# A two-layer network on one core: in each slot of the first layer, 16-block inverses go through DRAM, and decay products take two heads at once

## The reference, cut to what matters

```python
def step(S, inp):
    q_t, k_t, v_t, a_t, b_t = inp
    kS = jnp.einsum('bhd,bhdv->bhv', k_t, S)
    kkS = jnp.einsum('bhd,bhv->bhdv', k_t, kS)
    S = a_t[..., None, None] * (S - b_t[..., None, None] * kkS) + jnp.einsum('bhd,bhv->bhdv', k_t, v_t)
    o_t = jnp.einsum('bhdv,bhd->bhv', S, q_t)
    return (S, o_t)
```

## Time and profile before

| What | Value |
| --- | --- |
| Median of 3 runs | 1298.65 us |
| Lowest and highest run | 1297.44 and 1306.99 us |
| Profiled execution, span from first to last instruction | 1268.3 us |
| Profiled execution, own time outside the span | not given apart from the runs |
| Median less span | 30.35 us |

### The profile page before, as it was taken

The page is one execution under the profiler, slowest core; times in us unless marked ns, Lnnn a source line. Parts: engine busy times, 40 slices in busy tenths (PEclk is TensorE's granted clock), DMA queues, the critical chain, the costliest instruction groups (busy, mean ns, idle before and its releaser), DMA issues.

```text
span 1268.3 us, 36893 instructions
## 1 busy us (share of the span) xinstructions
PE 1107.3 (87%) x14528; PEld 793.9 (63%) x14528; DVE 906.1 (71%) x1818; ACT 797.2 (63%) x1467; POOL 595.0 (47%) x1213
## 2 busy tenths in 40 slices
PE   5768899999999999999989989986878877998991
PEld 1113576676677677677677677775545444798990
DVE  4865789998899999899977877884457566251232
ACT  3756888888998898897876766753334333332330
POOL 2434467667567667667655755654010005004404
PEclk9878999999999999999999999997699888998996
DMA  7012222222222212222223222412001104398982
GB/s 248 1 43 69 54 72 54 55 68 60 52 66 54 58 48 77 53 56 71 54 48 90 54 63 63 71 33 31 8 14 22 30 7 140 113 301 272 337 291 54
DMA packets 131662, 106.33 MB, mean 84 GB/s; under 512 B 60113, under 2 KB 119377, under 8 KB 131233
## 3 DMA queue, kind: packets, MB, share of 16 engines
q1 hardware_dynamic: 129440, 99.76, 27.9%
q0 software_dynamic: 2048, 4.20, 1.0%
HBM read 84.06 MB, written 15.73 MB: 79 GB/s over the span
## 4 chain that ended last, share of the span: by engine, by line
PE 51%; DVE 22%; issue 11%; POOL 6%; ACT 5%; DMA 2%; SPq 2%; DVEq 0%; POOLq 0%; ACTq 0%
PE bank L1052 6%; PE pair L732 5%; DVE vc L1499 4%; PE bank L1006 3%; PE bank L1059 3%; DVE AM L1569 3%; PE pair L696 3%; DVE kc L1499 3%; PE bank L834 2%; PE bank L784 2%; POOL xs L2007 2%; PE bank L879 2%; PE pair L850 2%; PE bank L773 2%; PE bank L826 2%
## 5 line engine op out<-in xcount | busy, mean ns | idle before, releaser
L1953 POOL TENSOR_TENSOR SU<-SU 128x14 f32<-128x14 f32 (+6 forms) x448 | 161.5, 360 | 34.9
L1957 POOL TENSOR_TENSOR SU<-SU 128x14 f32<-128x14 f32 (+6 forms) x448 | 147.5, 329 | 35.1
L1499 DVE SCALAR_TENSOR_TENSOR vc<-vy,conv,vc 128x512 f32<-128x512 f32 x192 | 152.2, 793 | 13.9 <-ACT vc L1194 13.5
L1499 DVE SCALAR_TENSOR_TENSOR kc<-ky,conv,kc 128x512 f32<-128x512 f32 x162 | 126.9, 808 | 10.7 <-ACT kc L1168 9.8
L2033 POOL TENSOR_TENSOR RR<-RR,nh 128x8 f32<-128x8 f32 x32 | 65.2, 2036 | 138.6 <-DVE RR L1641 138.5
L1839 DVE TENSOR_TENSOR vy<-bank,vc 128x512 f32<-128x512 f32 x46 | 31.8, 692 | 98.7 <-PE bank L1052 97.5
L732 PE MATMUL pair<-SM,KQ 64*128 64x128 f32 (+1 forms) x512 | 74.8, 369 | 18.1 <-DVE AM L1569 14.1
L1929 POOL TENSOR_TENSOR st<-st,nh 128x4 f32<-128x4 f32 x16 | 19.0, 1186 | 120.0 <-DVE st L1475 111.2
L696 PE MATMUL pair<-xnT,WQ 128*128 128x512 f32 x128 | 74.3, 663 | 0.2 <-DVE SM L1518 0.2
L664 PE MATMUL pair<-xnT,WQ 128*128 128x512 f32 x128 | 72.7, 653 | 1.5 <-ACT xnT L1156 0.8
L1802 DVE TENSOR_REDUCE SM<-pair 128x4 f32<-128x1024 f32 x32 | 39.1, 1222 | 41.5 <-PE pair L964 40.5
(11 more groups left out here) (315 smaller groups left out, 3190.6 us busy)
## 6 DMA issues: line engine op xcount, KB each, us to landing
AM<-in_wex_dram SPq DMA_DIRECT2D x32, 768.0 KB, 5.5
SM<-dscr SPq DMA_DIRECT2D x58, 256.0 KB, 3.7
V<-in_wex_dram SPq DMA_DIRECT2D x14, 768.0 KB, 5.0
et<-dscr SPq DMA_DIRECT2D x38, 256.0 KB, 3.7
SM<-fscr SPq DMA_DIRECT2D x64, 128.0 KB, 3.0
scratch<-AM SPq DMA_DIRECT2D x128, 48.0 KB, 1.8
SU<-scratch SPq DMA_DIRECT2D x256, 15.5 KB
xs<-idle SPq DMA_DIRECT2D x2, 1472.0 KB, 9.2
```

The costliest lines, as they stand in the source:

```text
L1499: e.scalar_tensor_tensor(c, y[:, :, k:k + 256], conv[:, ct, k:k + 1], c, ALU.mult, ALU.add).then_inc(s_c, 1)
L1953: e.tensor_tensor(tmp[:, 0:k, 0:15 - k], sub[:, 0:k, k:k + 1].to_broadcast([128, k, 15 - k]), sub[:, k:k + 1, k + 1:16].to_broadcast([128, ...
L1957: e.tensor_tensor(sub[:, 0:k, k + 1:16], sub[:, 0:k, k + 1:16], tmp[:, 0:k, 0:15 - k], ALU.subtract).then_inc(s_su, 1)
```

## The change

Four edits to the first layer's slot:

1. **Turning by DMA.** `inv_turn` and `inv_y0` go. SyncE gets `turned(n)`: it waits for the end of `substitute(n)` (and for the Y0 transfers of the unit before), writes SU's blocks to a new DRAM tensor `yscr` with 4 transfers, waits until they have landed, and reads them back into Y0 with 8 transfers, two for each group of 32 partitions. The reads fill only the diagonal 16-blocks of Y0, so the rest must be zero: a memset of Y0's second half is added to `substitute` ahead of step k = 7. It waits for `inv_w0` of the unit before. `turned(n - 1)` stands between `exponents(n + 1)` and `blocks(n)`. `inv_x0` waits for the 8 reads, and moves down behind the first tap of `vconv(2g + 1)`.
2. **Decay products of both heads at once.** The PSUM banks are renumbered so that banks 1 and 3 are the halves of one PSUM tensor, and `am` becomes three instructions of 128 x 1024 elements instead of six of 128 x 512. All waits on its semaphore are renumbered.
3. **The doubled copy on ScalarE.** `inv_w0` becomes two scaled copies of 128 x 256 elements on ScalarE, placed after `u2`. `inv_p1` becomes a multiplication of half as many elements by a number per partition. Masks shrink, and signs are moved so that `inv_s0` adds.
4. **GpSimd's order.** `scaled(g + 1)` always stands inside `substitute(g)`, ahead of k = 11, and so does a norm's power, where there is one, ahead of k = 9.

The small rest: one input fewer, two setup semaphores merged, two more memsets before the loop, and waits of the second layer's first units named anew for the renumbered banks.

```diff
-        bank = [D2[i // 2][:, 512 * (i % 2):512 * (i % 2) + 512] for i in range(4)]
+        bank = [D2[i % 2][:, 512 * (i // 2):512 * (i // 2) + 512] for i in range(4)]
...
-        NSU = 29
+        NSU = 30
...
             def blocks(n, new):
 
-                e.wait_ge(s_am, 6 * n + 6)
+                e.wait_ge(s_am, 3 * n + 3)
...
                 if n:
-                    e.wait_ge(s_i0, 3 * n - 2)
+                    e.wait_ge(l_y0, 128 * n)
...
+            def turned(n):
+
+                e.wait_ge(s_su, NSU * n + NSU)
+                if n:
+                    e.wait_ge(l_y0, 128 * n)
+                for a in range(4):
+                    e.dma_start(yscr[a], sub[32 * a:32 * a + 16, :, :]).then_inc(l_yw, 16)
+                e.wait_ge(l_yw, 64 * n + 64)
+                for a in range(4):
+                    for h in range(2):
+                        e.dma_start(Y0[32 * a + 16 * h:32 * a + 16 * h + 16, :, 16 * h:16 * h + 16],
+                                    yscr[a, 8 * h:8 * h + 8].rearrange("j r t -> r j t")).then_inc(l_y0, 16)
...
                 if n + 1 < NN: exponents(n + 1)
+                if n: turned(n - 1)
                 blocks(n, new and n + 1 < NN)
...
+            turned(NN - 1)
             for t in range(NTICK):
...
+            def inv_w0(n):
+                e.wait_ge(s_iy, 2 * n + 1)
+                if n:
+                    e.wait_ge(s_yfd, n)
+                e.activation(YP[:, :, 0:32], Y0[:, :, :], ACT.Copy, scale=minus_even32)
+                e.activation(YP[:, :, 32:64], Y0[:, :, :], ACT.Copy, scale=minus_odd32).then_inc(s_w0, 1)
...
-            def am(n, i):
-                part, hh = i // 2, i % 2
+            def am(n, part):
...
             def inv_x0(n):
-                e.wait_ge(s_i0, 3 * n + 2)
+                e.wait_ge(l_y0, 128 * n + 128)
                 e.transpose(X0[:, :, :], Y0[:, :, :]).then_inc(s_ix, 1)
...
             def inv_p1(n):
                 e.wait_ge(s_ia, 2 * n + 2)
-                e.tensor_tensor(PP[:, :, :], wide(bank[4]), lmask[:, :].unsqueeze(1).to_broadcast([128, NJ, 64]), ALU.mult).then_inc(s_ip, 1)
+                e.tensor_scalar(PP[:, :, 0:32], wide(bank[4])[:, :, 0:32], odd32, None, ALU.mult).then_inc(s_ip, 1)
...
                 for k in range(14, 0, -1):
-                    if late and k == 11:
+                    if k == 11 and n + 1 < NN:
                         scaled(n + 1)
+                    if k == 9 and key is not None:
+                        norm(key)
+                    if k == 7:
+                        if n:
+                            e.wait_ge(s_w0, n)
+                        c += 1
+                        e.memset(Y0[:, :, 16:32], 0.0).then_inc(s_su, 1)
```

More of the change, by code:

```diff
@@ L82, in program @@
         PP0 = sb("PP0", [128, NJ, 32])
-        bmask = sb("bmask", [128, 97])
-        mask16, mask32, odd16 = bmask[:, 0:32], bmask[:, 32:96], bmask[:, 96:97]
+        bmask = sb("bmask", [128, 5])
+        odd16, even16, odd32, minus_even32, minus_odd32 = (bmask[:, k:k + 1] for k in range(5))
         idle = sb("idle", [128, 512], BF16)
@@ L731, in gram @@
                             moved = KQ[hp:hp + 64, m, b, 1, s0:256] if k else KT2[hp:hp + 64, n % 2, b, s0:256]
-                            ins = e.matmul(bank[(3, 1)[hh]][:, part], KQ[hp:hp + 64, m, b, 0, s0:s0 + 128], moved, start=True, stop=True)
+                            ins = e.matmul(bank[2 * hh + 1][:, part], KQ[hp:hp + 64, m, b, 0, s0:s0 + 128], moved, start=True, stop=True)
                 ins.then_inc(s_gk, 1)
@@ L1437, in _ @@
                 if has_j: u2(j)
+                if has_i: inv_w0(i)
                 more(s, 7)
@@ L1896, in _ @@
                 if has_g: vconv(2 * g + 1, 0)
+                if has_i: inv_x0(i)
                 if has_e: lengths1(s // NG)
@@ L1905, in _ @@
                 if has_g: vconv(2 * g + 1, 2)
-                if has_i: inv_w0(i)
                 if has_i: inv_x1(i)
@@ L1938, in _, with substitute @@
             e.memset(PP0[:, :, :], 0.0).then_inc(s_zero, 1)
-            e.wait_ge(s_zero, 4)
-            def substitute(n, late):
+            e.memset(PP[:, :, :], 0.0).then_inc(s_zero, 1)
+            e.memset(Y0[:, :, :], 0.0).then_inc(s_zero, 1)
+            e.wait_ge(s_zero, 6)
+            def substitute(n, key):
                 c = NSU * n
@@ L2033, in _ @@
                     e.tensor_tensor(RR[:, 1, :, :], RR[:, 0, :, :], nh[:, :].rearrange("p (t h) -> p t h", t=4), ALU.pow).then_inc(s_r2, 1)
-                late = (g + 1) % NG == 0 and g + 1 < NN
-                if g + 1 < NN and not late: scaled(g + 1)
                 if s == 34:
@@ L2054, in _ @@
                     ins.then_inc(s_one, 1)
-                if gap(s + 1, "norm") is not None:
-                    norm(gap(s + 1, "norm"))
-                if g < NN: substitute(g, late)
+                if g < NN: substitute(g, gap(s + 1, "norm"))
+                elif gap(s + 1, "norm") is not None: norm(gap(s + 1, "norm"))
                 for k in range(10):
@@ L2085 @@
     s, t = r[:, None], r[None, :]
-    lm = np.zeros((128, 6, 64), f4)
-    for lv in range(6):
-        m = 1 << lv
-        a, b = (s % 64) // m, t[:, :64] // m
-        lm[:, lv, :] = (a % 2 == 1) & (b == a - 1)
-    lm[:, 0, :] = (s % 2 == 0) & (t[:, :64] == s % 64 + 1)
     sel = (np.arange(30)[None, :] - 14 == s // 64).astype(f4)
```

117 lines of the change are left out of this document (46 added, 71 removed).

## The result

| | Before | After |
| --- | --- | --- |
| Median | 1300.60 us of 4 runs (1297.44 to 1306.99) | 1495.88 us of 4 runs (1492.44 to 1503.75) |
| Ratio | | 1.152, 95% interval 1.147 to 1.157 |
| Span of the profiled run | 1268.3 us | 1492.6 us (own time of that run: 1494.35) |

The changed kernel is 15% slower. The ratio is the one on record, with its interval; the quotient of the two medians is 1.150. The forecast was 1515 us, in a range from 1430 to 1590.

The account below looks back on a forecast made before the run. TensorE sets the pace, but the SyncE and GpSimd chain has little room: 8.7 + 13.5 + 8.5 = 30.7 us a period instead of 23.9. 31 periods add 211 us, the last unit 5; span 1484 plus 30.35 gives 1515 us, range 1430 to 1590.

Parts of the forecast that it names:

- the signs named: First-layer loop: substitution starts 29 to 33 us apart, scratch writes directly behind yscr reads, X0 transpose waiting on DMA, TensorE about 75% busy.
- the 3.4 us of the forecast: Mean room per slot in the SyncE and GpSimd chain before the change: 23.9 - 8.7 - 11.8 us.
- the forecast's 11.8 us: GpSimd's mean substitution before the change, summed from its product and difference rows over 32 units.
- Last unit, start of its substitution to X0, more than before: End of the loop: short substitution of 10.5, transfers of 8.5 and 1.5, 20.5 us against 15.7, so 5 more.
- The bounds of the forecast, 5.5 and 10.3 us: SyncE's hand-over through yscr with the cheapest or the longest issues and landings, around the 8.5 us taken.
- the 0.4 that I had taken off for contention: GpSimd's substitution: steps faster beside an emptier VectorE, 0.4 us off, between 0 and 1.4.
- The forecast 28 us lower: Shared-port rule: removed VectorE products on Y0 and YP free 0.6 and 0.7 us a slot, substitution 12.6 us.
- Edits counted as nothing: VectorE's 3 us less and ScalarE's 0.9 us more a slot: no effect, since both engines wait for Y0.
- 7 us to spare: VectorE's path from Y0 reads to decay products: done after 23.6 us, while turned(n - 1) ends after 30.7.
- the rival's lower level: TensorE idles 7 to 8 us a slot, clock falls towards 1.2 GHz, about 1640 us; chance 0.10, shared with dearer transfers.
- the 7.5 from which it would decide: Added matmul time, in us, from which TensorE's slower clock would decide the time.
- the last of the sum: Whole kernel: adds 30.35 us, the median's excess over the span, to the forecast span of 1484, giving 1515 us.

Follow-up runs that it names:

- the three kernels above: Before with both heads' products in one instruction, plus halved inv_p1 (0.997), or doubled copy on ScalarE ahead of u2 (1.000), or all of these (1.002).
- turning_alone: Before with only the hand-over through DRAM, its Y0 memset, later inv_x0 and the small rest; 1462.81 us, ratio 1.128.
- products_only: Before with the decay products of both heads in one instruction, banks renumbered, and the small rest; 1294.06 us, ratio 0.998.
- changed_again: The changed kernel unaltered, run on chip 10 beside before at 1271.18 us; 1462.91 us, ratio 1.150.
- all_but_turning: The changed kernel with VectorE turning the blocks again and the full masked product inv_p1; 1328.22 us, ratio 1.023.

## Why the prediction was right, step by step

**What bounded the kernel, and what would be the bound: right.** Before, VectorE's work didn't set the pace: the three kernels above with less of it stay within 0.3% of before. That TensorE did rests on its 97 busy us of 100; no run took work from it. Of the signs named, SyncE's writes to scratch directly behind the reads, the transpose into X0 waiting for a DMA, and starts 29 to 33 us apart came as stated; TensorE is busy 81 of 100 us rather than 75. The room of the chain through SyncE and GpSimd was too small for one more link: the 3.4 us of the forecast minus the hand-over of 8 gives a loss, and `turning_alone` has it without any other edit. The room was really 2.9 us, 23.91 - 8.85 - 12.17: the forecast's 11.8 us leave out the first memset and `scaled` in the three slots where it stood inside.

**The terms of the period**, by the means of the trace of after:

| Term | Forecast | Measured |
| --- | --- | --- |
| Blocks, first write to the start of the substitution | 8.7 | 8.92 |
| Substitution | 13.5 | 13.22 |
| Hand-over, end of the substitution to the last read issued | 8.5 | 7.96 |
| of it: first write to first read | 3.2 | 4.27 |
| of it: eight reads | 5.2 | 3.66 |
| Period | 30.7 | 30.29 |
| Last unit, start of its substitution to X0, more than before | 5 | 4.7 |

The links close the period: 8.92 + 13.33 (the substitution without the last unit's short one) + 7.96 + 0.11 from the last read to the next write = 30.3.

The hand-over came out near its forecast by luck, only because two misses in it have opposite signs. The writes: I took 0.47 us to issue and 1.8 to land from line 495, whose rows bring 128 bytes a piece (32 numbers). Line 513, whose rows bring 64 bytes a piece, takes 0.602 us to issue and lands in 2.1: 3 x 0.60 + 2.1 = 3.9 by the medians, and the longest issue is 1.45 us. The reads: I took line 505's 0.65 as the nearest, and by the other bound 0.36; they take 0.43 in the median, 3.66 / 8 = 0.46 with their gaps. A transfer of line 505 brings 8 pieces of 1984 bytes into 8 partitions; one of line 517 brings 128 pieces of 64 bytes into 16 and is cheaper. So "few partitions" made a poor likeness; which number of the shape decides, no run separates. The bounds of the forecast, 5.5 and 10.3 us, hold the measured sum.

**The substitution.** `scaled` costs 1.285 us inside it, not 1.48, and the fourteen pairs take (146.5 + 32.2 + 155.8 + 35.1) / 32 = 11.55 us where they took 11.8. These are the groups, as the earlier trace rows:

```profile
L1962 POOL TENSOR_TENSOR SU<-SU 128x14 f32<-128x14 f32 (+6 forms) x448 | 155.8, 348 | 35.1
L1958 POOL TENSOR_TENSOR SU<-SU 128x14 f32<-128x14 f32 (+6 forms) x448 | 146.5, 327 | 32.2
```

```profile
L1970 POOL TENSOR_TENSOR SM<-KQ,SM 128x512 f32<-128x512 f32 x32 | 41.1, 1285 | 5.4 <-DMA SM<-fscr 5.4
```

So they are 0.3 us shorter, against the 0.4 that I had taken off for contention. The forecast 28 us lower, with 1.3 us freed, is not what happened. The rows show why. In the slot of the earlier trace rows the removed product on Y0 starts at 490.92 and the one on YP at 496.93:

```profile
490.92 0.61 DVE L1586 TENSOR_TENSOR Y<-PP,bmask 128x256 f32<-128x256 f32 x1
...
496.93 0.68 DVE L1608 TENSOR_TENSOR YP<-Y,bmask 128x512 f32<-128x512 f32 x1
```

The substitution had ended at 489.59 and the next starts at 498.61: there was no step for either to disturb. Over all 32 units of that trace, the product on Y0 never overlaps a step of a substitution, and the one on YP does so in two, by 0.03 us in all. What does disturb the steps is the convolution on VectorE, which takes two inputs from SBUF. In after's slot above, the difference on 54 columns takes 0.75 us at 523.97, beside line 1522 from 523.82 to 524.57, where the product on 54 columns ahead of it took 0.29; the last one, on only 14 columns, takes 0.76 us at 528.49, beside line 1522 from 528.44 to 529.17. Both end 0.1 us or so behind VectorE's instruction. Over the whole trace of after, 264 of the 896 steps overlap an instruction of line 1522; they take 0.51 us in the mean, the other 632 take 0.26. "SBUF — State Buffer", section "Who interferes with whom", of the Trainium skill says that a VectorE instruction with two inputs in SBUF contends with a GpSimd one that reads SBUF. By that rule the trace agrees on these pairs; where my lower forecast went wrong was in not asking which steps the removed instructions lay beside.

**Edits counted as nothing.** In the changed kernel this held, since VectorE waits 5.2 us for Y0 in each unit (166.6 / 32). VectorE's path from X0 to the end of the decay products grew from 22.3 us in the mean (22.1 in the slot of the forecast) to 23.9, and the writes to scratch follow them by 4.94 us in the mean, where I had 7 us to spare. But the price was nothing only behind that wait. Alone, the copy costs 13 us, and GpSimd's order 21 us, for which I had only looked at the chain. The prediction said "I count nothing for it, because in a slot of 30.7 us both engines wait for Y0 anyway", which is right for the sum and says nothing of the edit.

**The clock.** It fell to 0.88 in the loop, far from the rival's lower level. TensorE's time in a slot went from 23.2 to 0.806 x 30.29 = 24.4 us: 1.2 more, against the 7.5 from which it would decide.

**The step that failed** is the last of the sum: "to that come the 30.35 us by which the median lies above the span". A run's own time is 1.75 to 1.8 us above its span (1494.35 and 1492.6; 1293.53 and 1291.7 for `products_only`). So a span of 1268.3 belongs to a run of about 1270, which the runs of before on chip 10 show (1264.35 to 1278.41) and the three of the median, all above 1297, do not. The 30.35 us aren't time outside the span: some 23 of them are the second layer's, by the tails under `changed_again` (419.3 less 396.5), and 1.8 lie around the span. That the sum came out near the median was luck: the profiled run of after has the slower tail too, 418.7 us. Compared with the run whose tail is like that of the profile, the forecast span is 1484 and the measured one 1463.0: 21 us too many, of which 16 are the loop (199.8 where I had 216) and 5 the tail, 391.4 in place of 396.5.

**Still open.** A hand-over with room: a second tile SU, or the reads of yscr a whole slot later, might take it out of the ring of blocks and substitution. It wasn't tried, nor was issuing a part of the twelve transfers from another engine than SyncE. Open too is where the larger part of the 21 us of GpSimd's order in `all_but_turning` goes.

## What to carry to other kernels

An engine of low busy share can hold the ring that sets the pace: follow one unit through the in-order queues from its data to its data, add up issues and landings, and compare with the slot before work is moved there. When a step is put ahead of a wait in such a queue, or behind one, draw the ring again for everything queued behind it; the length of one ring goes one to one into the time, but a move can close a longer one. And a median and a profile are only added up if they are from the same set of runs: compare a run's own time with its own span first.

## What the runs showed of the hardware that I had not expected

- Issue times on SyncE don't follow the size of the transfer: 0.47 us for 48 KB in pieces of 128 bytes out of 32 partitions (line 495), 0.60 us for 16 KB in pieces of 64 bytes out of 16 partitions (line 513), 0.43 for 8 KB into 16 partitions (line 517), 0.60 for 15.5 KB in 8 pieces (line 505), whose time didn't change between the two kernels. Direction and shape differ together in these rows, so which of them counts is open.
- A small write to DRAM in pieces of 64 bytes lands in 2.1 us, up to 3.4, where one in pieces of 128 bytes lands in 1.8.
- In two sets of runs, on chips 13 and 10 by the record, before takes 1296 and 1271 us. For the changed kernel the loop's periods are the same in the slower and in the faster run, 30.29 and 30.24 us, and the tail differs by 27 us, in the stage that streams the experts' weights.
- A difference of the substitution on 14 columns takes 0.22 us in the earlier trace rows, and 0.76 in after beside one VectorE instruction with two inputs in SBUF.
